# Macaron block on Trainium2: both weighted FFN sums on VectorE in chunks of four tiles, with loads in pairs

## The reference

```python
x = x + 0.5 * ffn(layernorm(x), Wg, W1, b1, W2, b2)
x = x + attn(layernorm(x), mask, Wq, bq, Wk, bk, Wv, bv, Wo, bo)
x = x + 0.5 * ffn(layernorm(x), Wg, W1, b1, W2, b2)

def ffn(x, Wg, W1, b1, W2, b2):            # 8 experts, the best 2 of each row
    top_w, top_i = top_k(x @ Wg, 2); top_w = softmax(top_w)
    w = einsum(one_hot(top_i), top_w)      # weight of each expert, row by row
    return sum(w[..., i:i+1] * (gelu(x @ W1[i] + b1[i]) @ W2[i] + b2[i]) for i in range(8))
```

## Time and profile before

| quantity | value |
|---|---|
| time, median of 3 executions | 388.18 us (387.33 to 390.04) |
| the profiled execution | 387.34 us |
| its span, first to last instruction | 385.6 us |
| mean granted TensorE clock | 0.91 of full |
| TensorE busy | 312.6 us (81%) |
| VectorE busy | 228.4 us (59%) |
| ScalarE busy | 133.3 us (35%) |
| GpSimd busy | 241.6 us (63%) |
| line 821, VectorE, 32 instructions | 15.2 us busy, 513 ns each |
| line 424, GpSimd, 16 instructions | 11.5 us busy, 742 ns each |

### The profile page before, as it was taken

One profiled execution on the slowest core, in us unless ns is written; L12 is line 12 of the kernel. 1 busy time (PEld: TensorE's weight loads), 2 busy tenths in 40 slices (PEclk: granted clock), 3 DMA queues, 4 the chain that ended last, 5 costly groups with the idle time before them and its releaser, 6 DMA issues. The chain is left out here.

```text
span 385.6 us, 8340 instructions
## 1 busy us (share of the span) xinstructions
PE 312.6 (81%) x1964; PEld 247.8 (64%) x1970; DVE 228.4 (59%) x590; ACT 133.3 (35%) x375; POOL 241.6 (63%) x317
## 2 busy tenths in 40 slices
PE   2855699888888993899999999576798889989940
PEld 1832498887787871366677776333798788878820
DVE  5889364344333445979888889688244434333437
ACT  2205243332332335233455553333343223332322
POOL 5047567777777763564655556527677777777744
PEclk9997689999999997589999999655899999999995
DMA  7440466665555617000000000002476555555347
GB/s 210 139 122 2 109 153 192 159 164 163 135 155 162 164 48 218 2 0 0 15 14 14 12 9 20 24 7 60 126 194 166 154 159 152 152 155 156 111 146 202
DMA packets 35362, 41.88 MB, mean 109 GB/s; under 512 B 4808, under 2 KB 21840, under 8 KB 35344
## 3 DMA queue, kind: packets, MB, share of 16 engines
q1 hardware_dynamic: 30352, 31.44, 30.3%
q0 software_dynamic: 4992, 10.23, 8.8%
HBM read 33.39 MB, written 8.26 MB: 108 GB/s over the span
## 5 line engine op out<-in xcount | busy, mean ns | idle before, releaser
L401 POOL DMA_INDIRECT xg<-xn_rows,src_row x78 | 75.9, 973 | 33.3 <-issue 22.6
L408 POOL DMA_INDIRECT y_rows<-y_tile,dst_row x78 | 76.9, 985 | 24.0 <-issue 22.3
L1023 PE MATMUL banks<-xgT,w1b 128*128 128x128 f32 x624 | 89.1, 288 | 2.0 <-DMA w1b<-in_W1b 1.2
L768 DVE TENSOR_TENSOR h_pre<-banks,w1b 128x512 f32<-128x512 f32 x78 | 53.9, 691 | 58.4 <-PE banks L1023 57.0
L1032 PE MATMUL banks<-w,h_act 128*128 x624 | 87.1, 283 | 0.2
L1023 PEld LDWEIGHTS banks<-xgT,w1b 128*128 128x128 f32 x624 | 78.8, 198 | 4.9 <-DMA w1b<-in_W1b 1.4
L1032 PEld LDWEIGHTS banks<-w,h_act 128*128 128x128 f32 x624 | 75.5, 191 | 4.5 <-issue 0.8
L516 ACT COPY xgT<-banks 128x128 f32<-128x128 f32 x78 | 20.7, 265 | 125.7 <-PE banks L1042 125.7
L778 DVE COPY y_tile<-banks 128x128 f32<-128x128 f32 x78 | 22.7, 291 | 61.4 <-DMA y_rows<-y_tile,dst_row 55.5
L523 ACT ACTIVATE h_act<-h_pre 128x512 f32<-128x512 f32 x78 | 49.3, 632 | 5.8 <-DVE h_pre L768 5.8
L439 POOL TENSOR_TENSOR kv<-qk,vx 128x1024 f32<-128x1024 f32 x16 | 31.5, 1968 | 27.7 <-DVE qk L808 27.7
(11 more groups left out here) (182 smaller groups left out, 433.3 us busy)
## 6 DMA issues: line engine op xcount, KB each, us to landing
w1b<-in_W1b SPq DMA_DIRECT2D x78, 258.0 KB
y_back<-y_rows SPq DMA_DIRECT2D x16, 256.0 KB, 5.0
xg<-xn_rows,src_row POOLq DMA_INDIRECT x78
y_rows<-y_tile,dst_row POOLq DMA_INDIRECT x78
x<-in_L_attn_x SPq DMA_DIRECT2D x4, 256.0 KB, 3.8
xn_rows<-xn SPq DMA_DIRECT2D x4, 256.0 KB, 3.0
xn_rows<-xn_ring SPq DMA_DIRECT2D x16, 64.0 KB, 1.5
out<-x SPq DMA_DIRECT2D x4, 256.0 KB, 2.6
```

Of the source, the lines that this page charges most:

```text
L401: g.indirect_dma_start(out=xg[:, n % RING, :], out_offset=None, in_=xn_rows[f][:, :], in_offset=bass.IndirectOffsetOnAxis(ap=src_row[:, n: ...
L408: g.indirect_dma_start(out=y_rows[f][:, :], out_offset=bass.IndirectOffsetOnAxis(ap=dst_row[:, i:i + 1], axis=0), in_=y_tile[:, i % RING, ...
L768: v.tensor_tensor(h_pre[:, r, :].rearrange("p (c n) -> p c n", c=FC), h_bank(r).rearrange("p (c n) -> p c n", c=FC), w1b[:, r, DF:DF + FC] ...
L1023: last = mm(h_bank(q)[:, c * P:(c + 1) * P], w1b[:, q, c * P:(c + 1) * P], xgT[:, q, :], start=True, stop=True)
```

## The change

ScalarE's weighting (line 542) and GpSimd's addition (line 424) are gone, with the semaphore `y0_weighted`. VectorE does the first sum too, `x = y_back[:, 0] * half_w[:, 0] + x`, for the four tiles of a chunk in a row, and then the second sum `x = y_back[:, 1] * half_w[:, 1] + x` tile by tile. The semaphore `x_first` now counts VectorE's own first sums. SyncE issues the loads chunk by chunk, `k = 0` and then `k = 1`; before, the second chunk of `k = 0` was loaded ahead of the first of `k = 1`, and so on. GpSimd keeps `reciprocal_root`.

```diff
-                for k, c in ((0, 0), *((k, c + 1 - k) for c in range(NC - 1) for k in range(TOPK)), (1, NC - 1)):
-                    sp.dma_start(y_back[:, k, c * CH:(c + 1) * CH, :],
-                                 back_rows[k, :, c * CH:(c + 1) * CH, :]).then_inc(y_loaded[k][c], 16)
+                for c in range(NC):
+                    for k in range(TOPK):
+                        sp.dma_start(y_back[:, k, c * CH:(c + 1) * CH, :],
+                                     back_rows[k, :, c * CH:(c + 1) * CH, :]).then_inc(y_loaded[k][c], 16)
...
-            def add_first(f):
-                for t in range(0, NT, 2):
-                    if t % CH == 0:
-                        pool.wait_ge(b2_added, NC * f + t // CH + 1)
-                    pool.wait_ge(y0_weighted, NT * f + t + 2)
-                    g.tensor_tensor(y_back[:, 0, t:t + 2, :], y_back[:, 0, t:t + 2, :], x[:, t:t + 2, :],
-                                    ALU.add).then_inc(x_first, 1)
-                    if f == 0 and t == CH + 2:
-                        reciprocal_root(0, 0, CH)
-
             ffn_moves(0)
-            add_first(0)
+            reciprocal_root(0, 0, CH)
...
             ffn_moves(1)
-            add_first(1)
...
-                for t in range(NT):
-                    if t % CH == 0:
-                        act.wait_ge(y_loaded[0][t // CH], 16 * (f + 1))
-                    s.activation(y_back[:, 0, t, :], y_back[:, 0, t, :], ACT.Copy,
-                                 scale=half_w[:, 0, t:t + 1]).then_inc(y0_weighted, 1)
...
                 for t in range(NT):
-                    dve.wait_ge(x_first, (NT * f + t) // 2 + 1)
                     if t % CH == 0:
+                        dve.wait_ge(y_loaded[0][t // CH], 16 * (f + 1))
+                        dve.wait_ge(b2_added, NC * f + t // CH + 1)
+                        for u in range(t, t + CH):
+                            v.scalar_tensor_tensor(out=x[:, u, :], in0=y_back[:, 0, u, :],
+                                                   scalar=half_w[:, 0, u:u + 1], in1=x[:, u, :],
+                                                   op0=ALU.mult, op1=ALU.add).then_inc(x_first, 1)
                         dve.wait_ge(y_loaded[1][t // CH], 16 * (f + 1))
+                    dve.wait_ge(x_first, NT * f + t + 1)
                     v.scalar_tensor_tensor(out=x[:, t, :], in0=y_back[:, 1, t, :],
-                                           scalar=half_w[:, 1, t:t + 1], in1=y_back[:, 0, t, :],
+                                           scalar=half_w[:, 1, t:t + 1], in1=x[:, t, :],
                                            op0=ALU.mult, op1=ALU.add).then_inc(x_final if f else x_mid, 1)
```

More of the change, by code:

```diff
@@ L217, in macaron_kernel @@
         hi_ready, pair_ready, bias_split = sem("hi_ready"), sem("pair_ready"), sem("bias_split")
-        y0_weighted, x_first, inter_ps = sem("y0_weighted"), sem("x_first"), sem("inter_ps")
+        x_first, inter_ps = sem("x_first"), sem("inter_ps")
         hot_ready, back_ps, table_ready = sem("hot_ready"), sem("back_ps"), sem("table_ready")
```

## The result

The changed kernel takes 384.31 us (median of 19 executions, 382.86 to 387.08). The kernel before, timed beside it, takes 387.06 us (19 executions, 384.56 to 390.04), which is 1.1 us less than the three executions that the forecast started from. The ratio of the means is 0.9942, with a 95% interval of 0.9918 to 0.9965: 2.2 us less (1.4 to 3.2); the two medians lie 2.75 us apart. The forecast was 1.1 us less, 387.1 us, with a range from 384.9 us. Faster within 1% was right; the size was not, and the time lies outside the range.

A forecast was written before the change was run, and what follows sets the result against it. VectorE's second sums were taken to bound the end in FFN 1, and `phi` the start of attention after FFN 0. Gains of 0.6 + 0.5 = 1.1 us took 388.18 us to 387.1 us, range 384.9 to 389.7 us.

The forecast's parts named there:

- FFN 1, forecast 0.6 us: At the kernel's end, VectorE's last sum ends at 382.25 us against 382.82 us; bounds -1.2 to +0.5 us.
- GpSimd's disturbance: In FFN 1, VectorE's second sums lose 2.7 us to GpSimd's additions and waits for their results; the change ends this.
- The landing of the third load: In FFN 1, taken as unchanged at 375.8 us; VectorE's first sums of chunk 1 start from 375.85 us.
- FFN 0, forecast 0.5 us: At attention's start, `phi` goes at 159.5 us instead of 160.07 us, 0.55 us less, taken as 0.5; bounds 0 to -1.0 us.
- hangs on `phi`: At attention's start, everything from the outer products to the first product with `q` at 166.9 us depends on `phi`.
- is worth what `phi` moves: FFN 0's gain equals how much earlier `phi` goes, 0.55 us, passed down to the end as 0.5 us.
- The starting time: Time before the change, 388.18 us: median of three executions, 0.84 us above the profiled 387.34 us.
- A: Rival at attention's start: TensorE's clock comes up before 166 us; -1.6 us in all, some 0.5 us from the clock; 14%.
- B: Rival in attention: TensorE's clock stays at 1.2 GHz for one more attention tile; +2.1 us, 390.3 us; 9%.
- C: Rival in both FFNs: VectorE's sums don't overlap and each takes its full 0.34 us; +2.3 us, 390.5 us; 8%.
- D: Rival in both FFNs: an early store makes loads late for each chunk's second sums; +0.3 us, 388.5 us; 5%.

The follow-up runs named there:

- before_again: The kernel before without an edit, run again on chip 1 for a second profile; 1.0005 of the kernel before (0.9979 to 1.0030).
- late_warm: Changed kernel with TensorE's products on zeros ahead of attention started behind tile 4 of x, not tile 0; 0.9965 of the kernel before (0.9936 to 0.9993).
- after_again: The changed kernel without an edit, run again on chip 1 for a second profile; 0.9960 of the kernel before (0.9934 to 0.9985).

## Why the prediction was right or wrong

**The result's size.** Three measurements of the changed kernel against the kernel before gave 0.9942, 0.9960 and 0.9972. Weighted by their intervals that is 0.996, or 1.6 us; the stretches of the profiles show 1.3 to 1.5 us (0.9 or 1.1, and 0.4). The first measurement's 2.2 us has the 1.6 us inside its interval, and the repeats don't support the further 0.6 us. Within the first pair of profiles, 0.4 of the 2.1 us between the spans lie in FFN 1's slots and 0.3 us before FFN 0's first load, where the two programs do not differ.

**FFN 1, forecast 0.6 us: the mechanism was right, the size a little off.** Measured 0.4 us. The sums take 0.26 us each, 24 of them 6.39 us behind the third load (forecast 6.4), and GpSimd's disturbance is gone. The landing of the third load was the weak number. I took 5.1 us behind the issue of the first from one profile. In the seven profiles with the new sums and the new order it was 4.8 to 5.9 us, 5.35 us in the mean, and in the five where VectorE waited for it the last sum ends 6.4 us behind it. That is the missing 0.2 us.

**FFN 0, forecast 0.5 us: this step failed.** Measured 0.9 us at product 15 and 1.1 us at the logits. The forecast said that what follows "hangs on `phi`" and that FFN 0's part "is worth what `phi` moves". That rule held, and by a path that the forecast did not have. It had the end hang on product 0; but product 0 moves with the clock by up to 2.1 us between two profiles of one kernel, and product 1 keeps at most 0.5 us of it. What passes `phi`'s time on is this: the outer products of tile 0 start when `phi` is done, the 16th sum beside them takes 1.85 us in place of 0.33 us and ends just behind them, then come its statistics and the variance, GpSimd's second power, and `kv(1)`. So `kv(1)` stands 6.4 to 6.5 us behind `phi` in the old kernel and the new, and product 1 another 4.3 us behind. before_again showed the wait for `kv(1)` directly; that the long 16th sum belongs to the path is read from the rows, and no run took it away by itself. The path costs the forecast nothing by itself, since `kv(1)` moves as `phi` does (0.80 and 0.77 us).

What was wrong is the term's size. `phi` moved by 0.8 us, from 15.5 to 14.7 in the means, where I had 0.55: in the first changed profile it stands at 14.83 us, and the forecast's sums give 15.0, of which 0.1 us is a first load that landed at 2.8 and not 2.9 us; the repeats have it at 14.5 to 14.8. The rest, up to the 0.9 us at product 15, is the low clock of the one profile that I read, which put product 1 at 26.7 there and at 26.3 and 26.1 in the other two of the old form. The last 0.2 us, up to the logits, is within the scatter of that stretch.

**The starting time.** The time lies 2.8 us under the forecast, and most of this is not the change. The three executions' median was 388.18 us and 19 executions gave 387.06 us: this alone put the forecast 1.1 us too high. The gain was some 0.5 us more than the 1.1 us that I had. The further 1.2 us, up to the 2.75 us between the two medians, the repeats do not show. The range allowed for the scatter of single executions around my case, but not for a starting median that is itself high. That the sign and the order of size came out is the forecast's; that FFN 1's shortfall and FFN 0's excess partly cancel is luck.

**The rivals.** A, the clock comes up early: it was up for parts of the stretch in the first profile of the changed kernel, but also in before_again, and late_warm and after_again have the same logits with it early and with it low (105.2 and 105.3). The 0.5 us at which I had priced it is about the 0.4 us by which product 1 was late in the one profile of before. B, the clock stays low for one more attention tile: no profile has that; in after_again it came up at load + 20 us, ahead of product 0 at 20.9, and cost nothing. C, no overlap of the sums: refuted, four in 1.14 us. The Trainium skill (VectorE: DVE Perf Modes, "The DRAIN you can't avoid") says that the next operation starts only when the pipeline is empty, and also, which I had left out, that a next operation that is not held starts earlier; 0.26 us apart at a length of 0.34 us agrees with the second sentence and not with the first. D, late loads in the later chunks: not seen. VectorE waited 0 to 1.0 us for the third load, and from then on it had no gap.

## What to carry to other kernels

When a stage overlaps the next one, don't stop at the first instruction of the next stage that moves. Follow each engine's queue until the two paths meet for good; here that was the second product with `q`, and the first one, which varied most, passed almost nothing on. Distances that stay the same over all profiles show the path better than one profile's waits do. Moving work onto one engine can pay although that engine gets more to do, when the old split cost it waits and disturbed it, but each half of such a change (the order of loads, the place of the sums) may be worth little or nothing alone. And for an effect below 1%, take distances inside several profiles of each kernel: one pair of profiles, and one median of three, were both off by as much as the effect.

## What the runs showed of the hardware

- The same kernel took 385 to 387 us in two measurements and 426 to 427 us in two others (both on chip 1; the one at 385 us was on chip 8). In the two profiles of the kernel before the difference lies in the routing and the slots: 119.6 us from the logits to FFN 1's first load in one, 140.9 us in the other, with the additions and attention alike. Why is open.
- GpSimd's instructions do not all disturb VectorE alike. A sum beside the outer products took 1.85 us, ending with them (159.81 to 161.66 us, the outer products 159.52 to 161.52 us), and one that started inside the 1.08 us of the power took its usual 0.33 us (152.82 us). The Trainium skill (SBUF — State Buffer, "SBUF: two separate sides") says that a GpSimd instruction that reads SBUF and a VectorE one with two SBUF inputs exclude each other for a whole instruction; the first case agrees with it, the second doesn't. Whether the operation or its size makes the difference, no run here shows.
- Eight loads of 256 KB, issued in the same way, bring FFN 1's third one 4.8 to 5.9 us after the first issue in the paired order (ten profiles) and 4.6 to 5.3 us in the crossed order (four). It stays open whether the order does this.
